# Attention on one core: the shift rows of the next step are turned before the first run of value products instead of after it

## The chip, the cores and the metric

The kernel runs on one core of a Trainium2 chip. The core has five engines that work side by side: TensorE (PE; its weight loads are told apart as PEld), VectorE (DVE), ScalarE (ACT), GpSimd (POOL) and SyncE (SP), which here only issues DMAs. Each engine works through its own instructions in the order of the program, and engines wait for each other on semaphores. The metric is the device time of the whole program in microseconds; lower is better.

## The reference, cut to what matters

The program is two transformer layers on x of 4 x 1024 x 128: causal attention with 16 heads of 8 and a relative bias, a tree-routed feed-forward with wide attention, a second 16-head attention, and a gated feed-forward. The change lies in the first attention:

```
q = (x @ Wq.T + bq).reshape(b, n, h, hd).transpose(0, 2, 1, 3)
k, v = ...                                       # the same way
sim = jnp.einsum('bhid,bhjd->bhij', q, k)
bias = rel_emb[rp_bucket]
sim = sim + jnp.transpose(bias, (2, 0, 1)) * SCALE
causal = jnp.where(i[None, :] > i[:, None], -jnp.inf, 0.0).astype(sim.dtype)
attn = jax.nn.softmax(sim + causal, axis=-1)
out = jnp.einsum('bhij,bhjd->bhid', attn, v)
```

## The kernel before, in words

The stage is the function `attend_causal`. It takes 64 steps, n = 0 to 63, one for each head and batch (16 x 4). A step handles one 1024 x 1024 causal score matrix, of which only the lower triangle is computed. The order of the work is written out by hand for each engine; no scheduler changes it.

Four kinds of TensorE work make up a step, each a small function:

- `maxima(n + 2, i)`, i = 0 to 4 (lines 684 and 662): scores with the query on the partitions, two steps ahead, into one of two large PSUM buffers `psM`. VectorE reduces them to one maximum per query (line 582, eight reductions a step, the widest 1024 columns, those of part 2 being 256 and 768 columns). A part waits until the reductions of the part two before it have freed its buffer (`max_taken`).
- `rows(n + 1)` (line 698): VectorE has turned the maxima into negative shifts, in a high and a low bf16 half (`nm`, lines 592 and 594). One small matmul turns them from columns into 16 rows of 128. ScalarE copies these rows out of PSUM (`take_rows`, line 631, tile `mrow`), and SyncE sends them by DMA into two extra rows of the query tile of step n + 1 (`load_shifts`, line 469), so that the scores of that step come out already shifted.
- `scores(n, unit)`, unit 0 to 8 (lines 712 and 662): the shifted scores with the key on the partitions, 512 columns a unit. Unit 0 waits for the DMA of the shift rows (`r_loaded`). ScalarE takes the exponential of each unit (line 651, tile `probs`); GpSimd multiplies the parts near the diagonal by the bias (line 619).
- `values(n - 1, part)`, part 0 to 2 (lines 734 and 738): 13, 6 and 7 products of the probabilities of the step before with the values, summed in the one PSUM bank `psO`. After part 2, ScalarE copies the sum out (`take_o`, line 637) two steps late: between the exponentials of unit 0 and unit 1 of a later step.

The nine units of scores and the shift rows share **one ring of three PSUM banks** (class `Ring`, `psS`). The order in the ring is units 0, 1, 2, 3, then the rows, then units 4 to 8. Each entry may be written once the entry three before it has been taken by ScalarE. For the rows of step n + 1 that is **unit 1 of step n**; for unit 4 it is unit 2. Both functions say it with the same line:

```
if i >= 3:
    pe.wait_ge(slot_taken, i - 2)
```

`rows` has a second wait before this one, for `nm_ready` (line 594 on VectorE). The compiled program puts the wait on `slot_taken` in an instruction of its own of TensorE's sequencer (line 697), ahead of the weight load of line 698. `values(n - 1, 0)` has three waits of its own: the staged values, the near-diagonal multiplications of step n - 1, and the copy of the last head output but one.

SyncE issues in every step: four loads of query and key parts for step n + 4 (line 463), one store of a head output (line 473), two DMAs of the shift rows (line 469).

Of the kernel before, what the change touches and what calls it, by code (L numbers as in the profile page):

```python
# [475 lines left out]
def attend_causal(nc, m, g):  # L476
# [18 lines left out]
    def place(kb, qb):  # L495

        for unit, pieces in enumerate(PIECES):
            at = unit * CH
            for of, first, count in pieces:
                if of == kb and first <= qb * P < first + count:  # L500
                    return at + qb * P - first
                at += count
        raise AssertionError((kb, qb))
# [27 lines left out]
    with nc.Block() as block:  # L531
# [126 lines left out]
        def _(pe):  # L658
            def mask(out, r, table):

                for s in range(2):
                    done = pe.matmul(out, g["masks"][r:r + HALF, s, 0, :], g["masks"][r:r + HALF, s, table, :], start=False, stop=s == 1)  # L662
                return done

            def maxima(n, i):

                if n >= NG:
                    return
                u, k = n % BUFS, n * NM + i
                if k >= 2:  # L670

                    pe.wait_ge(max_taken, k - 1)
                if i == 0:
                    pe.wait_ge(s_loaded[u], (n // BUFS + 1) * 64)
                ps = psM[k % 2]
                at = 0
                for qb in MAXIMA[i]:
                    w = (qb + 1) * P
                    for bank in range(2):
                        a, z = max(at, bank * CH), min(at + w, (bank + 1) * CH)  # L680
                        if a >= z:
                            continue
                        r, ends = HALF * bank, z == at + w
                        last = pe.matmul(ps[:, a:z], qS[u][r:r + PROWS, qb * P:(qb + 1) * P], kS[u][r:r + PROWS, a - at:z - at], start=True, stop=not ends)  # L684
                        if ends:
                            last = mask(ps[:, z - P:z], r, 1)
                    at += w
                last.then_inc(maxima_done, 1)

            def rows(n):  # L690

                if n >= NG:
                    return
                i = ring.rows(n)
                pe.wait_ge(nm_ready, n + 1)
                if i >= 3:
                    pe.wait_ge(slot_taken, i - 2)
                pe.matmul(ring.bank(i)[0:SHIFTS * TPB, 0:P], nm[:, n % 2, :, :].rearrange("p s q -> p (s q)"), g["identb"][:, :],
                          start=True, stop=True).then_inc(slot_done, 1)

            def scores(n, unit):
                i, u = ring.index(n, unit), n % BUFS
                if unit == 0:
                    pe.wait_ge(r_loaded[u], (n // BUFS + 1) * 32)
                if i >= 3:

                    pe.wait_ge(slot_taken, i - 2)
                ps, r = ring.bank(i), ring.row(i)
                at = 0
                for kb, first, count in PIECES[unit]:  # L710
                    diagonal = first == kb * P
                    last = pe.matmul(ps[:, at:at + count], kS[u][r:r + RROWS, kb * P:(kb + 1) * P], qS[u][r:r + RROWS, first:first + count],  # L712
                                     start=True, stop=not diagonal)
                    if diagonal:
                        last = mask(ps[:, at:at + P], r, 2)
                    at += count
                last.then_inc(slot_done, 1)

            def values(n, part):

                if n < 0:
                    return
                if part == 0:
                    pe.wait_ge(v_staged, n + 1)
                    pe.wait_ge(near_done, (n + 1) * TPB)
                    if n > 0:
                        pe.wait_ge(o_taken, n)
                pr, v = probs[n % 2][:, :], v_ones[n % 3]
                for c, kb in VALUES[part]:
                    out = psO[c * VW:(c + 1) * VW, 0:2 * P]  # L730
                    far = place(kb, TPB - 1 - c)
                    if kb <= c:
                        a = place(kb, c)
                        last = pe.matmul(out.rearrange("p (q w) -> p q w", w=P), v[:, kb, :],  # L734
                                         bass.AP(pr.tensor, a, [list(pr.ap[0]), [far - a, 2], [1, P]]),
                                         start=kb == 0, stop=(c, kb) in ENDS, tile_position=(0, c * VW))
                    else:
                        last = pe.matmul(out[:, P:2 * P], v[:, kb, :], pr[:, far:far + P],  # L738
                                         start=False, stop=(c, kb) in ENDS, tile_position=(0, c * VW))
                if part == 2:  # L740
                    last.then_inc(pv_done, 1)
# [6 lines left out]
            for n in range(NG):  # L748
                scores(n, 0)
                scores(n, 1)  # L750
                maxima(n + 2, 0)
                maxima(n + 2, 1)
                scores(n, 2)
                scores(n, 3)
                values(n - 1, 0)
                rows(n + 1)
                scores(n, 4)
                maxima(n + 2, 2)
                scores(n, 5)
                scores(n, 6)  # L760
                maxima(n + 2, 3)
                values(n - 1, 1)
                scores(n, 7)
                scores(n, 8)
                maxima(n + 2, 4)
                values(n - 1, 2)
# [1238 lines left out]
```

## Time and profile before

| | |
|---|---|
| time, median of 3 runs | 1862.38 us (1860.15 to 1867.64) |
| time of the profiled execution | 1864.79 us |
| its span | 1863.1 us |
| busy over the span | PE 88%, DVE 81%, ACT 67%, POOL 42% |
| first attention stage | from about 70 to 506 us |

The span is the time from the first to the last instruction of the profiled execution. Busy shares are averages over stages with different limits, so the stage of the change has to be read by itself, in the windows and in the single steps.

### The profile page before, as it was taken

The numbers are of one execution on the slowest core, as the hardware profiler recorded it, in microseconds if no ns is written. First come the engines' busy times: TensorE is split into PE (matmuls) and PEld (weight loads), VectorE is DVE, ScalarE is ACT, GpSimd is POOL, SyncE is SP. The second block draws the span as 40 slices with busy tenths as digits, with TensorE's granted clock in tenths as the row PEclk, the third lists the DMA queues.
The fourth block names the chain that finished last, engine by engine and source line by source line (L and its number), as shares of the span: only waits on it lengthen the run. The fifth ranks groups of instructions, "written<-read, shape, count | busy, mean of one in ns | idle before, by whom it ended". The sixth has DMA issues, their size and how long they took to land. (4 is left out here: it accounts for less than half of the span.)

```text
span 1863.1 us, 48171 instructions
## 1 busy us (share of the span) xinstructions
PE 1636.9 (88%) x19058; PEld 1045.2 (56%) x19082; DVE 1517.5 (81%) x2250; ACT 1255.1 (67%) x2481; POOL 773.8 (42%) x1489
## 2 busy tenths in 40 slices
PE   5499999999745999999999639999999999999835
PEld 3266766776544887877677413444444444444424
DVE  7599999999444999988555769999999999999354
ACT  7378888888623444454333627988988988988734
POOL 4388888888635001000000123444444444444345
PEclk9599999999865999999999867999999999999967
DMA  8422222222171755573000351111111111111041
GB/s 270 161 77 87 86 84 87 86 85 84 44 157 26 103 93 89 94 90 59 1 1 0 122 188 40 56 58 53 55 59 54 54 59 54 54 59 48 20 102 46
DMA packets 132965, 141.87 MB, mean 76 GB/s; under 512 B 22989, under 2 KB 106122, under 8 KB 132746
## 3 DMA queue, kind: packets, MB, share of 16 engines
q1 hardware_dynamic: 132314, 138.79, 29.3%
q8 instruction: 148, 2.42, 0.5%
q14 instruction: 71, 0.58, 0.1%
q10 hardware_dynamic: 432, 0.07, 0.0%
HBM read 92.70 MB, written 44.98 MB: 74 GB/s over the span
## 5 line engine op out<-in xcount | busy, mean ns | idle before, releaser
L852 DVE TENSOR_REDUCE heads_mx<-heads_psM 128x1 f32<-128x1024 f32 x512 | 602.3, 1220 | 37.8 <-PE heads_psM L941 21.8
L921 ACT ACTIVATE heads_probs<-heads_psS 128x512 f32<-128x512 f32 x1024 | 546.0, 601 | 76.6 <-PE heads_psS L964 70.6
L890 POOL TENSOR_TENSOR heads_masked<-heads_probs,g_tri 128x128 f32<-128x128 f32 x512 | 233.7, 456 | 359.6 <-ACT heads_probs L921 359.5
L619 POOL TENSOR_TENSOR heads_probs<-heads_probs,one_ebias 128x256 f32<-128x256 f32 (+1 forms) x512 | 341.6, 690 | 82.1 <-ACT heads_probs L651 81.6
L651 ACT ACTIVATE heads_probs<-heads_psS 128x512 f32<-128x512 f32 x576 | 316.4, 603 | 65.9 <-PE heads_psS L662 60.7
L582 DVE TENSOR_REDUCE heads_mx<-heads_psM 128x1 f32<-128x1024 f32 (+7 forms) x512 | 349.6, 750 | 10.7 <-PE heads_psM L662 9.7
L941 PE MATMUL heads_psM<-heads_kS,heads_qS 48*128 48x512 bf16 x1024 | 229.9, 394 | 27.7 <-DMA heads_kS<-k_parts 18.8
L964 PE MATMUL heads_psS<-heads_qS,heads_kS 50*128 50x512 bf16 x1024 | 237.5, 388 | 0.7 <-ACT heads_probs L921 0.3
L1486 ACT ACTIVATE trees_hid_hi<-trees_hid 128x512 fp32r<-128x512 f32 x192 | 121.7, 634 | 153.3 <-DVE trees_hid L1507 151.8
L1507 DVE SCALAR_TENSOR_TENSOR trees_hid<-trees_psH,g_b,trees_chosen 128x512 f32<-128x512 f32 x192 | 144.0, 750 | 32.5 <-DMA trees_chosen<-leaf_choice 14.7
L684 PE MATMUL heads_psM<-heads_kS,heads_qS 48*128 48x512 bf16 (+3 forms) x768 | 147.8, 335 | 22.1 <-DMA heads_kS<-k_parts 19.2
L989 PE MATMUL heads_psO<-heads_probs,heads_ones_only 128*32 128x128 f32 x1920 | 161.8, 283 | 0.0
L990 PE MATMUL heads_psO<-heads_probs,heads_v_ones 128*32 128x128 f32 x1920 | 155.7, 273 | 0.0
L734 PE MATMUL heads_psO<-heads_probs,heads_v_ones 128*32 128x256 f32 x1280 | 150.9, 396 | 2.3 <-POOL heads_probs L619 2.0
L983 PE MATMUL heads_psO<-heads_probs,heads_ones_only 128*32 128x256 f32 x1280 | 148.7, 390 | 0.0
L712 PE MATMUL heads_psS<-heads_qS,heads_kS 50*128 50x512 bf16 (+3 forms) x768 | 141.4, 334 | 7.3 <-DMA heads_qS<-heads_mrow 5.4
L738 PE MATMUL heads_psO<-heads_probs,heads_v_ones 128*32 128x128 f32 x2048 | 136.6, 279 | 0.0
L1514 DVE SCALAR_TENSOR_TENSOR trees_hid_lo<-trees_hid,trees_hid_hi 128x512 fp32r<-128x512 f32 x192 | 134.2, 699 | 0.1
L964 PEld LDWEIGHTS heads_psS<-heads_qS,heads_kS 50*128 50x128 bf16 x1024 | 69.5, 93 | 114.3 <-ACT heads_probs L921 55.0
L1600 POOL COPY wide_qs<-two_qkT 128x1024 f32 (+1 forms) x4 | 4.2, 1039 | 282.6 <-SPq L1544 179.6
L983 PE MATMUL heads_psO<-heads_probs,heads_v_ones 128*32 128x256 f32 x768 | 120.9, 394 | 0.0
L989 PEld LDWEIGHTS heads_psO<-heads_probs,heads_ones_only 128*32 128x32 f32 x1920 | 72.5, 108 | 81.9 <-issue 81.8
(248 smaller groups left out, 3125.0 us busy)
## 6 DMA issues: line engine op xcount, KB each, us to landing
heads_qS<-q_parts SPq DMA_DIRECT2D x256, 96.0 KB
heads_kS<-k_parts SPq DMA_DIRECT2D x256, 96.0 KB
trees_chosen<-leaf_choice SPq DMA_DIRECT2D x96, 256.0 KB
head_outputs<-heads_oT SPq DMA_DIRECT2D x128, 128.0 KB
heads_qS<-heads_mrow SPq DMA_DIRECT2D x256, 4.0 KB
q_parts<-open_parts SPq DMA_DIRECT2D x8, 384.0 KB, 3.7
k_parts<-open_parts SPq DMA_DIRECT2D x8, 384.0 KB, 4.9
q_parts<-proj_parts SPq DMA_DIRECT2D x8, 384.0 KB, 3.3
```

What stands on the lines that cost most here:

```text
L582: last = dve.tensor_reduce(mx[:, p, qb:qb + 1], psM[(n * NM + i) % 2][:, at:at + w], AXX, ALU.max)
L619: pool.tensor_tensor(pr[:, a:a + w], pr[:, a:a + w], bass.AP(eb.tensor, eb.offset + NEAR - 1, [list(eb.ap[0]), [-1, w]]), ALU.mult).then_i ...
L651: act.activation(probs[n % 2][:, slot * CH:(slot + 1) * CH], ring.bank(i)[:, :], ACT.Exp).then_inc(slot_taken, 1)
L734: last = pe.matmul(out.rearrange("p (q w) -> p q w", w=P), v[:, kb, :], bass.AP(pr.tensor, a, [list(pr.ap[0]), [far - a, 2], [1, P]]), sta ...
L852: dve.tensor_reduce(mx[:, n % 2, k:k + 1], psM[k % 2][:, :], AXX, ALU.max, negate=True).then_inc(max_taken, 1)
L890: pool.tensor_tensor(masked[n % 2][:, kb, :], probs[n % 2][:, kb, kb * P:(kb + 1) * P], g["tri"][:, 0:P], ALU.mult).then_inc(near_done, 1)
L921: act.activation(probs[n % 2][:, kb, h * CH:(h + 1) * CH], ring.bank(i)[:, :], ACT.Exp).then_inc(slot_taken, 1)
L941: last = pe.matmul(psM[k % 2][:, h * CH:(h + 1) * CH], qS[u][r:r + PROWS, k * P:(k + 1) * P], kS[u][r:r + PROWS, h * CH:(h + 1) * CH], sta ...
L964: pe.matmul(ring.bank(i)[:, :], kS[u][r:r + RROWS, kb * P:(kb + 1) * P], qS[u][r:r + RROWS, h * CH:(h + 1) * CH], start=True, stop=True).t ...
L983: pe.matmul(out.rearrange("p (q w) -> p q w", w=P), v_ones[v][:, kb, :] if kb < c else ones_only[:, :], both, start=kb == 0, stop=False, t ...
L989: pe.matmul(out[:, 0:P], ones_only[:, :], pr[:, c, :], start=False, stop=False, tile_position=(0, c * VW))
L990: pe.matmul(out[:, P:2 * P], v_ones[v][:, kb, :], pr[:, b, :], start=False, stop=False, tile_position=(0, c * VW))
```

## The change

One line moves. In the loop over the steps, `rows(n + 1)` now stands before `values(n - 1, 0)`:

```
                 scores(n, 2)
                 scores(n, 3)
+                rows(n + 1)
                 values(n - 1, 0)
-                rows(n + 1)
                 scores(n, 4)
                 maxima(n + 2, 2)
```

The number of instructions of every engine stays the same, and the orders of VectorE, ScalarE, GpSimd and SyncE are unchanged. On TensorE it holds for the 62 steps n = 1 to 62: in step 0 there are no value products to be moved past, and in step 63 there are no rows. TensorE at the end of unit 3 of the scores and up to unit 4, before (heads_nm are the shifts, heads_psO the value products, heads_psS the ring):

```order
L712 MATMUL heads_psS<-heads_qS,heads_kS 128x128
L662 MATMUL heads_psS<-g_masks 128x128 x2
L734 MATMUL heads_psO<-heads_probs,heads_v_ones 32x256 x4
L738 MATMUL heads_psO<-heads_probs,heads_v_ones 32x128
L734 MATMUL heads_psO<-heads_probs,heads_v_ones 32x256 x3
L738 MATMUL heads_psO<-heads_probs,heads_v_ones 32x128 x5
L698 MATMUL heads_psS<-g_identb,heads_nm 16x128
L712 MATMUL heads_psS<-heads_qS,heads_kS 128x512
L662 MATMUL heads_psS<-g_masks 128x128 x2
```

The same place with the change:

```order
L712 MATMUL heads_psS<-heads_qS,heads_kS 128x128
L662 MATMUL heads_psS<-g_masks 128x128 x2
L698 MATMUL heads_psS<-g_identb,heads_nm 16x128
L734 MATMUL heads_psO<-heads_probs,heads_v_ones 32x256 x4
L738 MATMUL heads_psO<-heads_probs,heads_v_ones 32x128
L734 MATMUL heads_psO<-heads_probs,heads_v_ones 32x256 x3
L738 MATMUL heads_psO<-heads_probs,heads_v_ones 32x128 x5
L712 MATMUL heads_psS<-heads_qS,heads_kS 128x512
L662 MATMUL heads_psS<-g_masks 128x128 x2
```

The small matmul of line 698 moves past 13 value products; all 13 now stand behind it and behind its waits. ScalarE, on which the matmul of line 698 waits and which takes its result, has this order in both kernels: six exponentials (units 4 to 8 and the next step's unit 0), the copy of a head output, three exponentials (units 1 to 3), the copy of the shift rows, and again:

```order
L651 ACTIVATE heads_probs<-heads_psS 128x512 x6
L637 ACTIVATE heads_oT<-heads_psO 128x256
L651 ACTIVATE heads_probs<-heads_psS 128x512 x3
L631 ACTIVATE heads_mrow<-heads_psS 16x128
L651 ACTIVATE heads_probs<-heads_psS 128x512 x6
```

Nothing moves there: the copy of the head output stands ahead of the exponential of unit 1, and the copy of the shift rows behind that of unit 3.

## Rows read from the trace of the kernel before

**Rows 1.** The page: span, and busy time of each engine

```profile
span 1863.1 us, 48171 instructions
PE 1636.9 (88%) x19058; PEld 1045.2 (56%) x19082; DVE 1517.5 (81%) x2250; ACT 1255.1 (67%) x2481; POOL 773.8 (42%) x1489
```

**Rows 2.** Windows of the stage: length, busy time by engine, clock, DMA share, GB/s

```profile
110.00:480.00 370.00, 364.61 (x6301) 258.84 (x6301) 360.42 (x578) 310.68 (x636) 317.03 (x521) 1.00 0.27 84
```

**Rows 3.** Waits in the window 110 to 480: total us, times, longest us

```profile
PEld heads_psS L712 <- ACT heads_probs L651: 21.4, 115, 0.2
PEld heads_psS L712 <- DMA heads_qS<-heads_mrow: 14.7, 38, 1.0
...
DVE heads_mx L582 <- PE heads_psM L662: 4.7, 15, 0.5
PEld heads_psS L712 <- issue: 4.0, 20, 0.2
```

**Rows 4.** Timeline of ScalarE, steady step: start, us, instruction, idle before it

```profile
410.17 0.27 ACT L631 ACTIVATE heads_mrow<-heads_psS 16x128 bf16<-16x128 f32 x1
...
413.99 0.60 ACT L651 ACTIVATE heads_probs<-heads_psS 128x512 f32<-128x512 f32 x1 [0.26 <-PE heads_psS L662]
...
414.49 0.38 ACT L637 ACTIVATE heads_oT<-heads_psO 128x256 f32<-128x256 f32 x1
414.75 0.61 ACT L651 ACTIVATE heads_probs<-heads_psS 128x512 f32<-128x512 f32 x1
...
415.70 0.63 ACT L651 ACTIVATE heads_probs<-heads_psS 128x512 f32<-128x512 f32 x1
416.45 0.27 ACT L631 ACTIVATE heads_mrow<-heads_psS 16x128 bf16<-16x128 f32 x1
416.88 0.60 ACT L651 ACTIVATE heads_probs<-heads_psS 128x512 f32<-128x512 f32 x1 [0.16 <-PE heads_psS L662]
```

**Rows 5.** Timeline of TensorE's weight loads in the same step

```profile
413.45 0.10 PEld L712 LDWEIGHTS heads_psS<-heads_qS,heads_kS 50*128 50x128 bf16 x2 [0.20 <-issue]
...
414.64 0.11 PEld L712 LDWEIGHTS heads_psS<-heads_qS,heads_kS 50*128 50x128 bf16 x2
...
415.08 0.16 PEld L734 LDWEIGHTS heads_psO<-heads_probs,heads_v_ones 128*32 128x32 f32 x8
...
415.97 0.12 PEld L738 LDWEIGHTS heads_psO<-heads_probs,heads_v_ones 128*32 128x32 f32 x4
416.08 0.09 PEld L698 LDWEIGHTS heads_psS<-g_identb,heads_nm 128*16 128x16 bf16 x1
416.34 0.09 PEld L712 LDWEIGHTS heads_psS<-heads_qS,heads_kS 50*128 50x128 bf16 x1 [0.17 <-ACT heads_probs L651]
```

**Rows 6.** The sequencer's wait ahead of line 698, in the microsecond from 415

```profile
L697 PEldq EVENT_SEMAPHORE  x1: 51/51/51, 415.4 to 415.4; - x1
```

**Rows 7.** Weight load behind the second run of value products, same step

```profile
418.39 0.11 PEld L712 LDWEIGHTS heads_psS<-heads_qS,heads_kS 50*128 50x128 bf16 x3 [0.21 <-ACT heads_probs L651]
```

**Rows 8.** Step 0, rows straight behind scores: timeline of weight loads

```profile
86.84 0.09 PEld L698 LDWEIGHTS heads_psS<-g_identb,heads_nm 128*16 128x16 bf16 x1 [0.20 <-issue]
```

**Rows 9.** The maxima of part 2 and the shifts: TensorE and VectorE, same step

```profile
414.81 0.17 DVE L594 SCALAR_TENSOR_TENSOR heads_nm<-heads_mx,heads_nm 128x8 bf16<-128x8 f32 x1
...
416.92 0.27 PE L662 MATMUL heads_psM<-g_masks 64*128 64x128 bf16 x2
...
417.24 0.42 DVE L582 TENSOR_REDUCE heads_mx<-heads_psM 128x1 f32<-128x256 f32 x1
```

**Rows 10.** A step whose shift rows land late: weight loads, then VectorE

```profile
420.56 0.10 PEld L712 LDWEIGHTS heads_psS<-heads_qS,heads_kS 50*128 50x128 bf16 x2 [1.03 <-DMA heads_qS<-heads_mrow]
...
424.35 0.42 DVE L582 TENSOR_REDUCE heads_mx<-heads_psM 128x1 f32<-128x256 f32 x1 [0.49 <-PE heads_psM L662]
```

**Rows 11.** Timeline of SyncE, same step as Rows 4

```profile
415.23 0.58 SPq L473 DMA_DIRECT2D head_outputs<-heads_oT  x1
416.74 1.37 SPq L469 DMA_DIRECT2D heads_qS<-heads_mrow  x2
```

More of the change, by code:

```diff
@@ L754, in _ @@
                 scores(n, 3)
+                rows(n + 1)
                 values(n - 1, 0)
-                rows(n + 1)
                 scores(n, 4)
```

## The prediction

> **What bounds the kernel now.** The page comes first, but it only gives averages: TensorE is busy for 88% of the span and VectorE for 81% [rows 1]. The change touches one stage, so the second view is the window from 110 to 480 us, in which that stage runs steadily. There TensorE is busy for 364.6 and VectorE for 360.4 of 370 us, at a granted clock of 1.00 [rows 2]. The reader is to see that two engines are full together. Neither has room to hide what the other loses.
>
> The third view is the timeline of one undisturbed step. I call the weight load of its scores unit 0, at 413.45, its start [rows 5]. The copies of the shift rows of two steps in a row stand at 410.17 and 416.45 [rows 4]: a step takes 6.28 us. The path that sets this length goes as follows. Unit 0 is loaded at 413.45, its exponential runs from 413.99 to 414.59, and unit 3 of the scores, which needs that bank, is loaded at 414.64, 0.05 us after the exponential's end. The value products follow at 415.08, the rows at 416.08, unit 4 at 416.34 [rows 4, 5]. Then come the maxima of part 2. Their last matmul ends at 417.19 and VectorE starts to reduce them at 417.24 [rows 9], again 0.05 us later, the delay of a hand-over. So VectorE takes this part the moment TensorE has it. What comes later than now on this stretch of TensorE makes the step longer.
>
> A step that is disturbed confirms this. In it unit 0 waited for the DMA of its shift rows: the idle time before its load is 1.03 us, against 0.20 us in the undisturbed step. That is 0.83 us late, and VectorE then idled 0.49 us before the same 256-column reduction, although its idle time is hidden in part by the overlap of one reduction with the next [rows 5, 10].
>
> **The waits for the shift rows.** In the window, 38 weight loads of unit 0 waited for that DMA, 14.7 us in sum. 20 more show only 0.20 us each, put down to issue: this is what the change from value products to scores costs TensorE in any case. So the late DMAs cost 14.7 - 38 x 0.20 = 7.1 us in 58 steps [rows 3], or 7.6 us over the 62 steps that change. This is the only reserve from which the change could pay back.
>
> **What the change adds.** Nothing is added to any engine's work; a wait gets another place. The rows of step n + 1 go into the PSUM bank of unit 1. Its exponential stands behind the copy of a head output (414.49) and runs from 414.75 to 415.36 [rows 4]. The sequencer's wait of line 697 shows at 415.4, for 51 ns [rows 6]: it is over when that exponential is over, and not sooner. Today this costs nothing, because the 13 value products, from 415.08 to beyond 416, are already handed to TensorE ahead of it; the rows' load follows at 416.08, after 0.6 us of further cover [rows 5]. With the change nothing covers it. Behind the waiting instruction stand all 13 value products, unit 4 of the scores and the maxima of part 2. For unit 4 ScalarE waits, and then GpSimd; for the maxima VectorE waits. The other wait of the rows, for the shifts, doesn't matter: line 594 ends at 414.98 [rows 9].
>
> The cost, step by step:
> - The rows' load can start at 415.36 + 0.05 = 415.41 if the hand-over is as short as elsewhere, and at 415.45 with the 51 ns of the sequencer's wait. I take 415.45.
> - The value products' first load follows. In the trace the rows' load comes at 416.08, within the last loads of value products (415.97 for 0.12), and no idle time stands between them [rows 5]: the two kinds follow each other without a change-over. The matmul itself is small. I take 0.06 us. The other end is a full change-over of 0.20 us, as in step 0, where the rows stand straight behind scores [rows 8].
> - So the value products start at 415.51 instead of 415.08: 0.43 us later. The ends are 415.42 (0.34) and 415.65 (0.57).
> - Behind the value products unit 4 now follows directly. Today it is 0.24 us from the last value load's end (416.09) to 416.34, with the rows between; behind the second run, where nothing stands between, the idle time is 0.21 us [rows 5, 7]. This gives back some 0.02 us.
>
> Net: about 0.41 us a step, with ends of 0.32 and 0.55. The nearest row for each of the uncertain parts is in the same step, so the value is taken near the lower half. Over 62 steps: 62 x 0.41 = 25.4 us, with ends of 20 and 34.
>
> The Trainium skill bears on the second item. Its page "TensorE: Matmul & The Clock Gate", section "Architectural detail: the array is 16× 32×32, not 1× 128×128", says that TensorE's queue is a partial reorder window and can pull weight loads ahead of matmuls in flight. By it the loads of the value products could be done while the rows wait. In the undisturbed step the first value load (415.08) does not run ahead of the scores in front of it; no row here shows such a load under a wait. This rule is the third rival below.
>
> **What the change gives back.** The copy of the shift rows is now at 416.45, though the exponential before it in ScalarE's order started at 415.70 and ends at 416.33 [rows 4]: it waited for the rows' matmul. With the change the matmul is done by about 415.7, and the copy can follow the exponential, 0.12 us or somewhat more earlier. SyncE is free by then: its store ended at 415.81, and the DMAs of the rows start at 416.74, after the copy [rows 11]. They gain 0.12 us on their start. And the next step starts 0.41 us later, so they have 0.53 us more in which to land. The longest wait of a step exceeded the 0.20 us by about 0.8 us [rows 3, 10], and the mean over the 38 is 7.1 / 38 = 0.19 us. Most of these waits therefore vanish. Of the 7.6 us I take 7 us back, with ends of 5.5 and 7.6. This is relief that the added wait buys itself, not a gain on top of an unchanged step.
>
> **The sum.** +25.4 - 7 = +18.4 us. Against the profiled execution, 1864.8 us (span 1863.1), this gives 1883; against the median of the runs, 1862.4, it gives 1881. The ends are 62 x 0.32 - 7.6 = +12 and 62 x 0.55 - 5.5 = +29: 1874 to 1891. Nothing else in the program moves, so no other stage takes part.
>
> **The rivals.**
>
> *Faster, because the wait is free and only the early rows count.* If the bank were free when TensorE comes to the rows, at about 415.08, the order would cost nothing; the copy would come 0.12 to 0.25 us earlier and take away more than half of the 7.6 us of DMA waits, and the change-over saves 62 x 0.02 = 1 us. That gives 1862 - 7 = 1855. It decides from the point at which unit 1's exponential ends before the third unit of the scores is through. Against it stand its end at 415.36 and the sequencer's wait at 415.4 [rows 4, 6]. Chance 0.04.
>
> *No change that can be told, because something absorbs half of the delay.* VectorE has about 9.6 us of idle time in the window, 0.16 us a step, in which some of the delay might vanish, and ScalarE has more. Then perhaps 0.2 us a step would be left: 62 x 0.2 = 12, less 7, is +5: 1868. Against it speaks that the reductions of part 2 start 0.05 us behind their matmul [rows 9] and that most of the 9.6 us are waits for TensorE and fixed hand-overs. Chance 0.10.
>
> *Slower, but less, because the value products' loads run under the wait.* A value load takes about 0.11 us, and this is the most it saves: 62 x 0.30 = 18.6, less 7, is +12: 1874. Chance 0.10.
>
> *Slower by more, because TensorE's queue has run dry.* Behind the wait the change-over of 0.20 us comes in full, and the next sequencer's wait, that of the value products, adds its 0.05 us: 0.60 us a step, +37 - 6 = +31: 1893. For it speaks the row of step 0 [rows 8], which is a change from scores to rows and not from rows to values. Chance 0.08.
>
> **How the numbers follow.** The forecast has 0.68, the other two slower ones 0.10 and 0.08, no change 0.10, faster 0.04. A measurement of this kernel can tell about 0.5% (9.3 us) from no change, so slower means over 1871.7 and faster below 1853.1. Slower: 0.68 + 0.10 + 0.08 = 0.86; within: 0.10; faster: 0.04. The range leaves out the faster case, part of the one without change, and the top of the dearest: 1869 to 1892.
>
> **What the profile of the changed kernel would show.** The weight load of the rows stands about 2.0 us behind that of unit 0 (now 2.63), the first value load about 2.06 us behind it (now 1.63), and idle time of TensorE stands before the rows' load, about 0.3 us, ended by ScalarE's line 651. The 256-column reduction of VectorE shows idle time, released by TensorE, in nearly every step instead of in 15. The step is about 6.7 us long, and the waits for the shift rows' DMA fall from 38 to a few. The window of the stage ends some 18 us later; the stages behind it have their lengths of before. The forecast is wrong if the value products' first load stays near 1.63 us behind unit 0, or if the step stays at 6.28 us although the wait is there: then TensorE was not what VectorE waited for.

## The result, and the profile after

| | before | after |
|---|---|---|
| median of five runs | 1862.38 us (1860.15 to 1867.64) | 1886.10 us (1885.64 to 1888.51) |
| span of the profiled execution | 1863.1 us | 1884.3 us |

The changed kernel is slower: ratio 1.0126, 95% interval 1.0107 to 1.0144. The forecast was 1881 us (1869 to 1892). It had the direction and the mechanism of the loss right, the cost of a step too low, and the reason for the relief only in part.

The stage in the window 110 to 480 us (length, busy time of PE, PEld, DVE, ACT and POOL, granted clock, DMA share, GB/s):

```profile
110.00:480.00 370.00, 350.68 (x5938) 247.86 (x5939) 341.98 (x546) 284.10 (x601) 298.28 (x492) 1.00 0.26 81
```

Every engine is busy for less time than in [rows 2] and gets through less work (the ends of matmuls are modelled, so the figure for PE is the roughest): VectorE runs 546 instructions here instead of 578. The clock is still 1.00, so the loss is in waits. The waits in the same window (total us, times, longest us):

```profile
ACT heads_probs L651 <- PE heads_psS L662: 81.5, 164, 1.0
POOL heads_probs L619 <- ACT heads_probs L651: 71.7, 109, 1.0
PEld heads_psS L698 <- DVE heads_nm L594: 27.3, 55, 0.5
DVE heads_mx L582 <- PE heads_psM L662: 24.2, 54, 0.5
PEld heads_psS L712 <- issue: 21.3, 107, 0.2
PE heads_psS L698 <- ACT heads_probs L651: 19.3, 55, 0.4
...
PEld heads_psS L712 <- DMA heads_qS<-heads_mrow: 0.5, 2, 0.3
```

Three lines answer to [rows 3]. Line 698, which waited for nothing before, now waits in every step (55 times), 0.5 us each for its weight load. VectorE waits for TensorE 54 times instead of 15. The wait for the shift rows' DMA has gone from 38 times to 2. One name misleads: the load of line 698 is put down to VectorE's line 594, because its own semaphore is that one; the matmul of the same line is put down to ScalarE's line 651. The timeline decides between them. ScalarE in one step (it answers to [rows 4]):

```profile
412.18 0.25 ACT L631 ACTIVATE heads_mrow<-heads_psS 16x128 bf16<-16x128 f32 x1
...
416.78 0.60 ACT L651 ACTIVATE heads_probs<-heads_psS 128x512 f32<-128x512 f32 x1 [0.26 <-PE heads_psS L662]
...
417.27 0.38 ACT L637 ACTIVATE heads_oT<-heads_psO 128x256 f32<-128x256 f32 x1
417.53 0.60 ACT L651 ACTIVATE heads_probs<-heads_psS 128x512 f32<-128x512 f32 x1
...
418.49 0.63 ACT L651 ACTIVATE heads_probs<-heads_psS 128x512 f32<-128x512 f32 x1
418.96 0.25 ACT L631 ACTIVATE heads_mrow<-heads_psS 16x128 bf16<-16x128 f32 x1
420.17 0.60 ACT L651 ACTIVATE heads_probs<-heads_psS 128x512 f32<-128x512 f32 x1 [0.95 <-PE heads_psS L662]
```

And TensorE's weight loads in that step (they answer to [rows 5]):

```profile
416.24 0.10 PEld L712 LDWEIGHTS heads_psS<-heads_qS,heads_kS 50*128 50x128 bf16 x2 [0.20 <-issue]
...
418.25 0.09 PEld L698 LDWEIGHTS heads_psS<-g_identb,heads_nm 128*16 128x16 bf16 x1 [0.50 <-DVE heads_nm L594]
418.38 0.19 PEld L734 LDWEIGHTS heads_psO<-heads_probs,heads_v_ones 128*32 128x32 f32 x8
...
419.63 0.09 PEld L712 LDWEIGHTS heads_psS<-heads_qS,heads_kS 50*128 50x128 bf16 x1 [0.20 <-issue]
```

VectorE's shifts and its first reduction of part 2 (they answer to [rows 9]):

```profile
417.60 0.17 DVE L594 SCALAR_TENSOR_TENSOR heads_nm<-heads_mx,heads_nm 128x8 bf16<-128x8 f32 x1
...
420.53 0.42 DVE L582 TENSOR_REDUCE heads_mx<-heads_psM 128x1 f32<-128x256 f32 x1 [0.43 <-PE heads_psM L662]
```

The shifts are ready at 417.77, unit 1's exponential ends at 418.13, the rows' load starts at 418.25: it is the exponential that ends the wait. The copies at 412.18 and 418.96 are a step apart: 6.78 us instead of 6.28.

For the comparisons below I took the same points from every step of a trace, behind unit 0's weight load, as medians over 55 steps. All times are in us. The column of waits is the sum of what 54 step lengths exceed the shortest by, so it holds every delay that is not in each step; nearly all of it is waiting for the shift rows' DMA. The arrival is the median time from the start of ScalarE's copy to the last arrival signal of the DMA; it shifts by up to 0.05 us with the choice of the steps.

| kernel | unit 1's exp. ends | rows' load | first value load | unit 4's load | step | waits for DMA | arrival |
|---|---|---|---|---|---|---|---|
| before | 1.904 | 2.629 | 1.624 | 2.884 | 6.282 | 6.97 | 3.22 |
| after | 1.902 | 2.016 | 2.141 | 3.389 | 6.787 | 0.24 | 2.80 |
| e1_wait_only | 1.903 | 2.959 | 1.954 | 3.215 | 6.614 | 1.44 | 2.93 |
| e2_waits_first | 1.902 | 2.016 | 2.049 | 3.278 | 6.673 | 0.87 | 3.04 |
| e3_after4 | 1.904 | 2.019 | 1.624 | 2.885 | 6.280 | 2.13 | 3.21 |
| e3_after8 | 1.904 | 2.193 | 1.624 | 2.884 | 6.281 | 2.24 | 3.31 |
| e7_copy_first | 1.902 | 2.016 | 2.141 | 3.389 | 6.787 | 0.56 | 2.81 |
| e9_before_copy | 1.903 | 2.903 | 1.898 | 3.158 | 6.554 | 4.30 | 3.04 |
| e8_after4_copy | 1.903 | 2.142 | 1.899 | 3.159 | 6.560 | 0.57 | 3.06 |
| f1_copy_idle | 1.626 | 1.739 | 1.865 | 3.113 | 6.511 | 0.42 | 3.16 |
| e10_store_behind | 1.904 | 2.629 | 1.624 | 2.884 | 6.280 | 0.51 | 2.84 |
| f2_all | 1.626 | 1.867 | 1.624 | 2.884 | 6.280 | 0.05 | 2.82 |

From unit 4's load to the end of the step it is 3.395 to 3.401 us in all twelve kernels (6.282 - 2.884 before, 6.787 - 3.389 after). So what an edit does to the step is done before unit 4.

### The profile page after: what moved, and what is told of

Read it like the earlier page. It is cut to its first block and busy times, and to the rows that moved or that the text cites. A ratio compares the mean times of both kernels' runs of the same rounds, so it can differ in the third digit from the quotient of the medians.

```text
span 1884.3 us, 48171 instructions
## 1 busy us (share of the span) xinstructions
PE 1643.2 (87%) x19058; PEld 1047.7 (56%) x19082; DVE 1519.1 (81%) x2250; ACT 1244.6 (66%) x2481; POOL 772.8 (41%) x1489
## 5 line engine op out<-in xcount | busy, mean ns | idle before, releaser
L684 PE MATMUL heads_psM<-heads_kS,heads_qS 48*128 48x512 bf16 (+3 forms) x768 | 149.5, 334 | 21.5 <-DMA heads_kS<-k_parts 18.4
```

## The experiments

The ratios of the experiments compare with runs of the kernel before that were made beside them. Its median there was 1864.7 us for e1, e2 and e3, 1864.2 us for e7 to e10, and 1865.3 us for f1 and f2, some 2 to 3 us above the 1862.38 us from which the prediction and the expected times start. A measured time is therefore best read by its ratio.

### e1_wait_only: the wait without the move

```
                 scores(n, 3)
+                if 1 <= n < NG - 1:
+                    pe.wait_ge(slot_taken, ring.rows(n + 1) - 2)
                 values(n - 1, 0)
                 rows(n + 1)
```

> The order of the kernel before (rows behind the first run of value products), with one wait added: in steps 1 to 62 the first run of value products also waits until ScalarE has taken unit 1 of the scores, as the rows do ahead of it in the changed kernel. Theory W (the wait for unit 1's exponential is the whole loss, the place of the small matmul costs nothing): the first value load comes 2.02 to 2.10 us behind unit 0's instead of 1.62, the step is 6.68 to 6.76 us where its shift rows are in time, and the waits for their DMA stay near 7 us in sum, because the rows come no earlier within the step: 1887 to 1893 us. Rival P (the loss is TensorE changing between scores, rows and value products): the step stays at 6.28 us and the time at 1862 us.

Measured: 1877.45 us, ratio 1.0067 (1.0050 to 1.0084). One step's weight loads:

```profile
312.61 0.10 PEld L712 LDWEIGHTS heads_psS<-heads_qS,heads_kS 50*128 50x128 bf16 x2 [0.20 <-issue]
...
314.56 0.16 PEld L734 LDWEIGHTS heads_psO<-heads_probs,heads_v_ones 128*32 128x32 f32 x8 [0.43 <-ACT heads_probs L651]
...
315.57 0.09 PEld L698 LDWEIGHTS heads_psS<-g_identb,heads_nm 128*16 128x16 bf16 x1
```

The value products come 0.330 us later than before (1.954 against 1.624) and the step is 0.332 us longer: the step pays for a delay of the value products one to one. So the wait alone makes two thirds of the 0.505 us, with the rows where they were. The rest of the value products' delay is 0.187 us: in the changed kernel the rows' load comes 0.062 us later than the load that waits here, and the first value load another 0.125 us behind it. Rival P expected an unchanged step of 6.28 us and is out as the main cause. My own numbers were off too: 1877 us is well under the 1887 to 1893 us that I had. The value products' load came 0.05 us behind the exponential, sooner than I had put it, because here the load itself carries this wait. And the waits for the DMA did not stay near 7 us: they fell to 1.4, although the copy stands as far from the next unit 0 as before (6.614 - 3.327 = 3.29 us, before 3.29). This second miss led to e10.

### e2_waits_first: the value products' own waits ahead of the rows' waits

```
+                if n >= 2 and n < NG - 1:
+                    value_waits(n - 1)      # v_staged, near_done, o_taken
                 rows(n + 1)
                 values(n - 1, 0)            # for these steps without its waits
```

> The changed kernel, but the three waits of the first run of value products stand ahead of the rows' two waits. In the changed kernel the first value load comes 0.125 us behind the rows' load. Theory W2 (0.05 us of this or more is the value products' own sequencer wait, which runs after the rows' wait instead of beside it): the distance shrinks to 0.03 to 0.07 us, the step from 6.79 to about 6.72 us, the time to about 1882 us. Rival P (TensorE changing from rows to value products takes the 0.125 us): nothing moves, 1886 us. If the waits of both only line up one behind the other in another order, rows' load comes later and the time is 1886 too.

Measured: 1881.57 us, ratio 1.0087 (1.0070 to 1.0104).

```profile
314.46 0.09 PEld L698 LDWEIGHTS heads_psS<-g_identb,heads_nm 128*16 128x16 bf16 x1 [0.50 <-POOL heads_v_ones L610]
314.49 0.37 PEld L737 LDWEIGHTS heads_psO<-heads_probs,heads_v_ones 128*32 128x32 f32 x11
```

The distance from the rows' load to the first value load shrinks from 0.125 to 0.033 us, and the step from 6.787 to 6.673. So 0.09 us of the 0.114 us was the value products' wait, which the sequencer can only begin once the rows are through: in the changed kernel the two sequencer waits run one after the other, 51 ns each.

```profile
L697 PEldq EVENT_SEMAPHORE  x1: 51/51/51, 418.2 to 418.2; - x1
...
L727 PEldq EVENT_SEMAPHORE  x1: 51/51/51, 418.3 to 418.3; - x1
```

(These two are from the changed kernel, in the step shown above.) The change of TensorE from the rows to the value products costs no more than the 0.033 us that are left, so of rival P next to nothing remains. The other 0.02 us of the step are gained between the first value load and unit 4 (1.229 us instead of 1.248); why is open.

### e3_after4 and e3_after8: rows inside the first run of value products

```
                 for at, (c, kb) in enumerate(VALUES[part]):
+                    if between is not None and at == 4:     # e3_after8: 8
+                        rows(between)
...
-                values(n - 1, 0)
-                rows(n + 1)
+                values(n - 1, 0, n + 1)
```

> The rows stand inside the first run of value products, behind its first 4 of 13. Theory W: these 4 keep TensorE busy for about 0.25 us of the wait, so the step loses what is left: 0.2 to 0.3 us instead of 0.50, a step of 6.48 to 6.58 us; the waits for the shift rows' DMA nearly vanish. 1868 to 1874 us. Rival P (changing between rows and value products costs by itself, and here it happens twice): 6.8 us or more a step, 1886 us or more.

> The rows stand inside the first run of value products, behind its first 8 of 13. Theory W: the 8 cover the wait to its end (about 2.02 us behind unit 0's load), so the step stays at 6.28 us, while the copy of the shift rows comes 0.2 to 0.27 us earlier in it (2.73 to 2.8 instead of 3.00 us) and the waits for their DMA shrink from about 7.6 us to 2 or 3: 1856 to 1859 us, faster than both kernels. Rival P (changing costs by itself): slower than before, 1866 us or more.

Measured: 1860.66 us, ratio 0.9974 (0.9965 to 0.9984), and 1861.08 us, ratio 0.9975 (0.9964 to 0.9987). Both are faster than before, by a quarter of a per cent. The rows behind 4 products:

```profile
314.76 0.10 PEld L712 LDWEIGHTS heads_psS<-heads_qS,heads_kS 50*128 50x128 bf16 x2 [0.20 <-issue]
...
316.38 0.16 PEld L738 LDWEIGHTS heads_psO<-heads_probs,heads_v_ones 128*32 128x32 f32 x8
316.77 0.08 PEld L698 LDWEIGHTS heads_psS<-g_identb,heads_nm 128*16 128x16 bf16 x1 [0.24 <-issue]
316.81 0.12 PEld L738 LDWEIGHTS heads_psO<-heads_probs,heads_v_ones 128*32 128x32 f32 x3
```

And the matmuls of the same place (line 738 is line 734 of the other kernels):

```profile
316.38 0.64 PE L738 MATMUL heads_psO<-heads_probs,heads_v_ones 128*32 128x256 f32 x8
316.83 0.22 PE L698 MATMUL heads_psS<-g_identb,heads_nm 128*16 128x128 bf16 x1
```

The wait is as real here as in the changed kernel: the rows' load comes at 2.019 us, as there. It costs nothing: the loads of the first four products (eight records, two for each) take 0.16 us, but their matmuls 0.64 us by their modelled ends, and no idle time stands before the rows' matmul. My 0.2 to 0.3 us of loss with 4 products was wrong: I had read their cover off the weight loads, which run ahead of the matmuls. Changing between the two kinds of work twice costs nothing either, which speaks against rival P once more. With 8 products it came out as expected (1861.08 us is a little over my range, but the ratio lies inside it): the step stays, and the waits fall from 6.97 to 2.24 us. It is no better than with 4, because the copy of the shift rows stands behind unit 3's exponential in both (2.73 and 2.76 us behind unit 0's load).

### e7_copy_first, e8_after4_copy, e9_before_copy: a copy moved less far than meant

In the changed kernel, in e3_after4 and in the kernel before:

```
+                    if slot == 0 and n >= 2:
+                        take_o(n - 2)
                     act.activation(probs[n % 2][...], ring.bank(i)[:, :], ACT.Exp).then_inc(slot_taken, 1)
-                    if slot == 0 and n >= 2:
-                        take_o(n - 2)
```

> The changed kernel, but ScalarE copies the head output ahead of unit 0's exponential, in idle time, instead of between those of unit 0 and unit 1. Unit 1's exponential then ends about 1.64 us behind unit 0's weight load instead of 1.90. Theory W (this exponential alone ends TensorE's wait): the rows' load moves from 2.02 to about 1.75 us, the step from 6.79 to about 6.53 us; with 1 to 3 us of waits for the shift rows' DMA in 62 steps: 1869 to 1874 us. Rival P (changing between scores, rows and value products): step unchanged, 1886 us.

> Rows behind 4 of the 13 value products, and ScalarE's copy of the head output ahead of unit 0's exponential. Theory W: TensorE has no wait left at the rows; the copy of the shift rows comes at about 2.5 us behind unit 0's load instead of 2.73, so the waits for their DMA (2.4 us in sum with the rows behind 4 products alone) shrink to under 1 us. Step 6.28 us, because VectorE's reductions and TensorE are both full at that length: 1855 to 1859 us. Rival: if VectorE is not full, the step itself gets shorter than 6.27 us and the time falls below 1853.

> The kernel before with only ScalarE's copy of the head output ahead of unit 0's exponential. Rows stay behind the value products, at 2.74 us behind unit 0's load, and their copy behind them at 3.00. Theory W: nothing moves by more than 0.3%, 1860 to 1865 us: it was not unit 1's exponential that this order waited for. If it is faster by 4 us or more, the value products or unit 2 to 4 waited for ScalarE somewhere that the timeline did not show.

Measured: 1886.96 us (ratio 1.0121, 1.0103 to 1.0138), 1875.43 us (1.0052, 1.0036 to 1.0068) and 1876.34 us (1.0066, 1.0048 to 1.0084). None of the three came out as expected, because the edit did not do what it was meant to: the wait for unit 0's scores stood ahead of it in the program, so the copy ran after this wait, at the time of the exponential, and the exponential 0.28 us later (0.821 instead of 0.540 us behind unit 0's load). Unit 1's ended at 1.90 us as before.

They still tell something. Unit 3 of the scores needs unit 0's bank, and the value products follow it. Where nothing else held them (e9, e8) they came 0.274 and 0.275 us later and the step grew by 0.272 and 0.280 us. In e7, where they wait for unit 1 anyway, the same 0.28 us cost nothing: first value load 2.141 and step 6.787, both to the nanosecond those of the changed kernel. Two waits that run side by side don't add up; the later one is paid.

### f1_copy_idle: the copy moved ahead of that wait too

```
-                    act.wait_ge(slot_done, i + 1)
...
+                    if slot == 0 and n >= 2:
+                        take_o(n - 2)
+                    act.wait_ge(slot_done, i + 1)
                     act.activation(probs[n % 2][...], ring.bank(i)[:, :], ACT.Exp).then_inc(slot_taken, 1)
```

The cut lines are unit 0's wait for earlier value products. It goes too, since the copy begins with the same wait.

> The changed kernel, with ScalarE's copy of the head output ahead of unit 0's exponential and also ahead of its wait for unit 0's scores. (In the three kernels of the last call the copy stood behind that wait, so it ran no earlier and only pushed unit 0's exponential back by 0.28 us; unit 1's ended when it did before.) Now the copy runs in ScalarE's idle time, from about 0.2 us behind unit 0's weight load; unit 1's exponential ends at 1.64 us instead of 1.90. Theory W: the rows' load moves from 2.02 to 1.75 us, the step from 6.79 to 6.53 us; time 1869 to 1874 us. Rival P: step unchanged, 1886 us.

Measured: 1872.09 us, ratio 1.0035 (1.0022 to 1.0048). ScalarE and then the weight loads of one step (line 695 is line 698 of the other kernels):

```profile
315.43 0.39 ACT L637 ACTIVATE heads_oT<-heads_psO 128x256 f32<-128x256 f32 x1
315.80 1.59 ACT L650 ACTIVATE heads_probs<-heads_psS 128x512 f32<-128x512 f32 x3
```

```profile
315.26 0.10 PEld L709 LDWEIGHTS heads_psS<-heads_qS,heads_kS 50*128 50x128 bf16 x2 [0.20 <-issue]
...
317.00 0.09 PEld L695 LDWEIGHTS heads_psS<-g_identb,heads_nm 128*16 128x16 bf16 x1 [0.22 <-DVE heads_nm L594]
317.12 0.19 PEld L731 LDWEIGHTS heads_psO<-heads_probs,heads_v_ones 128*32 128x32 f32 x8
```

This is the cleanest test of the cause. The order on TensorE is that of the changed kernel, and only the moment at which unit 1's exponential ends is another: 0.276 us earlier. The rows' load moves by 0.277 us, the first value load by 0.276, the step by 0.276. The wait for this exponential is shown to be what the change pays for, but for the 0.09 us of the second wait (e2) and what little is left beside it.

### e10_store_behind: why a longer step took the DMA waits away

```
                 if n + 4 < NG:
                     load_s(n + 4)
-                if n >= 2:
-                    store_o(n - 2)
                 if n + 1 < NG:
                     load_r(n + 1)
+                if n >= 2:
+                    store_o(n - 2)
```

> The kernel before, but SyncE issues the store of the head output behind the DMAs of the shift rows instead of ahead of them. Theory Q (the shift rows' DMA stands in a queue behind the store and the part loads, which is why a longer step alone took the waits away in the run with only the wait added): the time from the copy's start to the arrival falls from 3.2 us to about 2.9 or less, the waits shrink from about 7.6 us to under 3, step 6.28: 1855 to 1859 us. Rival M (only the margin between copy and next step counts, the arrival does not depend on what else is under way): 1862 us, waits of about 7 us.

Measured: 1856.61 us, ratio 0.9961 (0.9947 to 0.9975), with f2_all the lowest ratio of all. SyncE and the waits in the window:

```profile
310.38 1.53 SPq L463 DMA_DIRECT2D heads_qS<-q_parts  x2
311.95 1.41 SPq L463 DMA_DIRECT2D heads_kS<-k_parts  x2
314.60 1.39 SPq L469 DMA_DIRECT2D heads_qS<-heads_mrow  x2
316.04 0.58 SPq L473 DMA_DIRECT2D head_outputs<-heads_oT  x1
```

```profile
PEld heads_psS L712 <- DMA heads_qS<-heads_mrow: 1.1, 3, 0.6
```

The copy of the shift rows stands where it stood before (2.997 us behind unit 0's load). Still the arrival falls from 3.22 to 2.84 us and the waits from 6.97 to 0.51 us. So the margin alone does not explain the waits (rival M).

The packets in the traces show what the two DMAs of 4 KB stand behind. These are medians over 55 steps, and times run from the start of the copy. Counted are the large packets that start between the copy and the last packet of the shift rows:

| kernel | store packets (1 KB) | load packets (2 KB) | last of these ends | last shift packet starts |
|---|---|---|---|---|
| before | 128 | 33 | 2.62 us | 2.73 us |
| e1_wait_only | 128 | 22 | 2.40 us | 2.43 us |
| after | 127 | 9 | 2.24 us | 2.39 us |
| e10_store_behind | 0 | 76 | 1.95 us | 2.43 us |

Before, the shift rows are through only when the large transfers that SyncE issued ahead of them are. It need not be the store: e10 takes the store away and has more load packets ahead, e1 and the changed kernel keep the store and have fewer of the loads. About 2.4 us is the earliest in all twelve traces, however soon the rest is done. The run that shows the cause is e10; the share of the loads is read from this order in time alone.

The loads are fewer in the changed kernel because SyncE issues its work in one sequence. The rows' DMAs are issued 0.29 us earlier in a step that is 0.5 us longer, so the last load of the round is issued by 0.64 us behind unit 0's load, where it was 1.43.

### f2_all: three edits together

The rows behind 4 products (e3_after4), the copy in idle time (f1_copy_idle) and the store behind (e10_store_behind), on the kernel before.

> Three edits on the kernel before: the rows behind 4 of 13 value products, the copy of the head output in ScalarE's idle time, and the store behind the shift rows' DMAs. TensorE then has no wait at the rows, and the shift rows arrive early. Theory: both sources of delay were gone in the run with the store behind alone, and what is left is the step of 6.28 us, which VectorE's own chain (6.27 us) also has: 1855 to 1858 us, no better than that run. Rival: TensorE alone sets 6.28 us and was held by unit 0's exponential; then nothing changes either, but if VectorE had room, a step under 6.27 us would be seen.

Measured: 1857.79 us, ratio 0.9964 (0.9950 to 0.9978). No better than e10 alone, as expected. The window shows why:

```profile
110.00:480.00 370.00, 369.65 (x6418) 260.62 (x6415) 364.21 (x588) 308.72 (x649) 323.28 (x531) 1.00 0.27 85
```

Next to no waits for the DMA are left (0.05 us), the rows wait for nothing, and the step is 6.280 us all the same. TensorE is busy throughout, and VectorE's idle time is mostly the fixed hand-overs between its dependent instructions. Which of the two sets the 6.28 us was not separated.

## Why the prediction came out as it did

**What bounds the kernel.** Right, and now shown for this stretch: 0.330 us of delay ahead of the value products gave 0.332 us of step (e1), 0.276 us less gave 0.276 us less (f1). No engine hid any of it. The rival "something absorbs half" is out.

**The wait.** Right. The rows' load came 2.016 us behind unit 0's; the prediction had 2.00. It is 0.114 us behind the exponential's end. In e1, where the first load behind the wait carries it itself, it is 0.051; the 0.063 us between them is about the 51 ns of the sequencer's own wait instruction. The prediction had 0.09 us from the exponential's end to the load, 0.02 us too little.

**The value products behind the rows.** Here the term was mis-sized. I took 0.06 us from the rows' load to theirs, because in [rows 5] the two kinds of load follow each other without idle time. Measured: 0.125 us. The row was read rightly for the change-over, 0.033 us (e2), but I left out the second sequencer wait, which before had run long ahead of its load. The bound of 0.20 us held it, but its source was weak: the row of step 0 [rows 8] lies in a stretch with a granted clock of 0.50, while the steady steps have 1.00. I had put this second wait, at 0.05 us, into the rival "TensorE's queue has run dry"; it is real, and the change-over of 0.20 us that this rival added is not. The measured 0.505 us a step lies midway between the forecast's 0.41 and that rival's 0.60.

**What unit 4 gets back.** 0.012 us, where I had 0.02.

**The step.** 0.517 - 0.012 = 0.505 us instead of 0.41; over 62 steps 31.3 us instead of 25.4.

**The waits for the shift rows' DMA.** The size was about right: 6.97 us fell to 0.24 over 54 step lengths, which is 7.7 us for 62; I had 7. The reason was only half right. I had them vanish because the copy comes earlier and the next step later. e1 has no such extra margin, and still lost four fifths of its waits; e10 lost nearly all of them by the order on SyncE. A good part of the relief came from the traffic: in a longer step less of it lies ahead of the shift rows (the packets under e10), and they arrive 2.80 us behind their copy instead of 3.22. The prediction left the arrival as it was, so that its 7 us fit is partly luck. The copy itself moved by 0.269 us (2.996 to 2.727), more than twice my 0.12, since it starts before the exponential ahead of it has ended. e3_after4 shows what an earlier copy is worth by itself: the step stays at 6.28, the arrival at 3.21 us, the margin grows by 0.27 us, and the waits fall to 2.13 us.

**The sum.** 31.3 - 7.7 = +23.6 us; the medians differ by 23.7. That these agree to 0.1 us is luck. The spans of the two profiled executions differ by 21.2 us only. Step 1 is 1.5 us shorter in that of the changed kernel (7.26 us against 8.76), and its stage starts 1.1 us earlier, for which the cause is open. The two together, 2.6 us, are about what the spans lack. In step 1 it is the granted clock, as the window from 90 to 96 us shows:

```profile
90.00:96.00 6.00, 6.00 (x65) 3.98 (x61) 5.49 (x9) 3.95 (x8) 4.78 (x8) 0.50 0.21 66
90.00:96.00 6.00, 5.64 (x94) 3.90 (x92) 5.86 (x10) 4.87 (x10) 5.18 (x10) 0.97 0.21 67
```

The first line is the kernel before, the second the changed one. This does not come from the order: e10_store_behind, with TensorE's order of before, has 0.91 and a step 1 of 7.23 us, and f1_copy_idle, with the changed order, 0.50 and 9.11 us.

The forecast of +18.4 missed by the 5.9 us of the mis-sized step and by less than 1 us of relief.

**The rivals.** Faster: out, the bank was never free. Slower but less, by loads that run under the wait: the first value load stood at least 0.125 us behind the rows' load in every one of the 55 steps, so nothing ran ahead under the sequencer's wait. In e3_after4 the loads do run ahead of matmuls in flight, as the Trainium skill says in "TensorE: Matmul & The Clock Gate", section "Architectural detail: the array is 16× 32×32, not 1× 128×128". The trace agrees: four products' loads take 0.16 us there and their matmuls 0.64 us. But the changed kernel has no load that ran ahead of a waiting sequencer.

## What to carry to other kernels

- A wait belongs behind work that is already handed over. The same wait stood in the kernel before, at the same moment, and cost nothing behind 13 products, or 4; in front of them it cost 0.5 us, 62 times. Before moving a small instruction forward, look up when its semaphore is released, not how long the instruction takes.
- If the next instruction has several waits of its own, count them: behind a wait that really held, the next one was paid on top (0.09 us here), while two waits that ran side by side did not add up (e7).
- Look at what a small, urgent DMA stands behind in its queue. Issuing one store after it instead of before gave 0.4%, where the best order on TensorE gave 0.3%. The intervals overlap, so which is better is not shown, and both together gave no more.

## What was not expected of the hardware

- Weight loads of the value products say little about how long these keep TensorE busy: four products, loaded from 1.62 us on, covered a wait until 2.02 us, while the next loads had otherwise followed at 1.87 us.
- A wait carried by a weight load let it start 0.051 us after the releasing exponential's end; one in a sequencer instruction of its own, 0.114 us after.
- Four different orders (before, e3_after4, e10, f2_all) have the same step to within 2 ns. In all four the first value load (1.624 us) and unit 4's load (2.884 to 2.885) stand at the same points, and TensorE and VectorE are both all but full.
